# Output product of the feed-forward part as split one-pass products with stationary weights, its tail in the next group, and loads two groups ahead

## The reference, cut to what matters

```python
x = _layernorm(x + mixer(x))          # inner width 256, 4 heads of 64
x = _layernorm(x + ffn(x))
# ffn, on tokens xf (8192 x 128), 16 experts of hidden width 64, one shared of width 128:
g = sigmoid(xf @ gate_w.T)
topv, topi = top_k(g, 4)
combine = zeros_like(g).at[rows, topi].add(topv / sum(topv))
hin = einsum('td,edh->eth', xf, e_win)
vin = einsum('td,edh->eth', xf, e_vin)
h = silu(hin) * vin * combine.T[:, :, None]
routed = einsum('eth,ehd->td', h, e_wout)
shared = silu(xf @ ws_in) * (xf @ vs_in) @ ws_out
ffn = shared + routed
```

## Time and profile before

| what | us |
|---|---|
| median of 3 runs (912.12 to 923.52) | 912.57 |
| profiled execution, its own time | 916.93 |
| its span, first to last instruction | 915.2 |
| TensorE busy | 823.2 |
| VectorE busy | 669.4 |
| GpSimd busy | 372.1 |
| ScalarE busy | 363.3 |
| mean granted TensorE clock, as a share of 2.4 GHz | 0.966 |

### The profile page before, as it was taken

The page is one execution under the profiler, slowest core; times in us unless marked ns, Lnnn a source line. Parts: engine busy times, 40 slices in busy tenths (PEclk is TensorE's granted clock), DMA queues, the critical chain, the costliest instruction groups (busy, mean ns, idle before and its releaser), DMA issues.

```text
span 915.2 us, 17726 instructions
## 1 busy us (share of the span) xinstructions
PE 823.2 (90%) x5783; PEld 643.9 (70%) x5783; DVE 669.4 (73%) x1759; ACT 363.3 (40%) x621; POOL 372.1 (41%) x372
## 2 busy tenths in 40 slices
PE   6879866799999999899989999999999999999966
PEld 5646655677777777777777777777777777777754
DVE  5899944577777777777786878777867777878654
ACT  4767742224343434333333443333434343433131
POOL 5040037253536262626262626353726353534200
PEclk8999977699999999999999999999999999999979
DMA  4877734300403040404030403040304040400000
GB/s 114 258 242 271 272 116 119 115 25 24 126 23 126 24 126 23 126 23 126 23 126 23 126 23 126 23 126 23 126 23 126 23 126 23 126 23 24 1 11 12
DMA packets 53104, 81.01 MB, mean 89 GB/s; under 512 B 10176, under 2 KB 36952, under 8 KB 49112
## 3 DMA queue, kind: packets, MB, share of 16 engines
q1 hardware_dynamic: 53080, 80.68, 28.2%
HBM read 55.24 MB, written 25.43 MB: 88 GB/s over the span
## 4 chain that ended last, share of the span: by engine, by line
PE 49%; DVE 17%; issue 14%; DMA 10%; POOL 5%; SPq 3%; ACT 2%; POOLq 1%; DVEq 0%; ACTq 0%
PE bank L1402 12%; DMA max_b<-max_scratch 7%; PE bank L1372 5%; PE bank L1376 5%; PE bank L1373 5%; PE bank L1392 4%; PE bank L1345 3%; DVE st L991 3%; PE bank L1321 3%; DVE acc L839 2%; PE bank L1319 2%; DVE Y L1003 2%; PE bank L1326 2%; DMA x_in<-in_L_attn_x_dram 2%; DVE out_sb L1003 2%
## 5 line engine op out<-in xcount | busy, mean ns | idle before, releaser
L755 ACT ACTIVATE s_in<-bank 128x512 f32<-128x512 f32 x144 | 85.9, 597 | 195.9 <-PE bank L1376 195.0
L1402 PE MATMUL bank<-ewout,h 128*128 128x128 f32 x1024 | 146.5, 286 | 0.0
L1402 PEld LDWEIGHTS bank<-ewout,h 128*128 128x128 f32 x1024 | 123.9, 191 | 25.4 <-issue 25.4
L554 POOL TENSOR_TENSOR rs<-ve,half 128x4 f32<-128x4 f32 x32 | 32.6, 1019 | 267.5 <-DVE ve L999 267.5
L1103 DVE TENSOR_TENSOR h<-s_in,bank 128x512 f32<-128x512 f32 x144 | 98.1, 681 | 58.5 <-PE bank L1376 50.3
L1372 PE MATMUL bank<-yT_hi,in_hi 128*128 128x512 f32 x288 | 128.2, 445 | 6.8 <-DVE h L1103 6.8
L1376 PE MATMUL bank<-yT_lo,in_hi 128*128 128x512 f32 x288 | 115.3, 400 | 0.0
L1373 PE MATMUL bank<-yT_hi,in_lo 128*128 128x512 f32 x288 | 114.6, 398 | 0.0
L540 POOL TENSOR_TENSOR D<-a_tok,max_b 128x512 f32<-128x512 f32 x64 | 65.4, 1043 | 118.5 <-DVE max_b L911 67.9
L1107 DVE TENSOR_TENSOR h<-h,bank 128x512 f32<-128x512 f32 x128 | 87.3, 682 | 19.8 <-PE bank L1392 19.8
L952 DVE TENSOR_TENSOR state<-kept,bank 64x130 f32<-64x130 f32 x128 | 36.6, 286 | 64.8 <-POOL kept L569 34.7
(11 more groups left out here) (197 smaller groups left out, 1634.2 us busy)
## 6 DMA issues: line engine op xcount, KB each, us to landing
xact_scratch<-xact SPq DMA_DIRECT2D x16, 1024.0 KB, 4.9
max_b<-max_scratch SPq DMA_DIRECT2D x15, 1024.0 KB, 7.7
xa<-xact_scratch SPq DMA_DIRECT2D x16, 512.0 KB, 6.4
silu_z<-xact_scratch SPq DMA_DIRECT2D x16, 512.0 KB, 3.8
inter_w<-inter_scratch SPq DMA_DIRECT2D x30, 256.0 KB, 7.0
x_in<-in_L_attn_x_dram SPq DMA_DIRECT2D x16, 256.0 KB, 4.9
xt_scratch<-x_t SPq DMA_DIRECT2D x16, 256.0 KB, 4.8
xT<-xt_scratch SPq DMA_DIRECT2D x16, 256.0 KB, 8.0
```

The costliest lines, as they stand in the source:

```text
L755: act.activation(s_in[:, j % 2], bank[4][:], ACT.Silu).then_inc(silu_done, 1)
L1402: i = pe.matmul(bank[7][:, k * P:(k + 1) * P], h2[:, j % 2, k * P:(k + 1) * P], w, start=(j == k == 0), stop=(j == NJ), skip_group_check=True)
```

## The change

- The output product has the weights as the stationary operand and h as the moving one: out^T = w^T h, in three one-pass products of 128x512 (`ffn_out_high`: out_hi x h_hi, out_lo x h_hi; `ffn_out_low`: out_hi x h_lo, a slot later), summed in bank 7. GpSimd splits the output weights in phase 1.
- h2 gets a ring of RB = 4 buffers. ScalarE makes its rounded part h_hi (`hidden_high`), GpSimd the rest h_lo (`hidden_low`), nine times a group each.
- The output is now transposed: ScalarE copies bank 7 to oT (`out_copy`), TensorE transposes it back (`out_tokens`), into bank 6. This tail, the sum with Y (kept by ScalarE in y_res), its statistics and its normalisation are done in the next call of `mix`: `ffn_sum` in slot 1, `ffn_statistics` in slot 2, `ffn_norm` in slot 6, ahead of the mixer step of that slot. So each group's result is stored one group later.
- The head's transposes use bank 5 instead of bank 7.
- The combine weights are split in two f32r parts instead of three bf16 ones (routing has eleven operations), with 128 rows in the combine product. `combine_rows(j - 1)` stands between the two halves of `ffn_in(j)` from slot 3.
- VectorE's slot order is h2(j - 1) first, then h1(j), but for slot 2.
- The skip products go from GpSimd to ScalarE. GpSimd's order is written out by hand anew, with the differences and masks of the two halves apart.
- `max_b` is loaded two groups ahead; the loop runs over groups 2 to 13, with 1 and 14 written out.

```diff
             def mix(g, f):        # SyncE
-                sp.wait_ge(arg_sub, nth(g, 4, 3))
-                if not (isinstance(g, int) and g == NG - 1):
-                    load_max(g + 1)
+                if not is_last(g):
                     sp.wait_ge(val_mm[1], g + 1)
...
+                if f is not None and before(f) is not None:
+                    store(before(f))
+                if not is_last(g, 2):
+                    sp.wait_ge(arg_sub, nth(g + 1, 4, 3))
+                    load_max(g + 2)
...
+                keep_state(0)
+                keep_state(1)
+                hidden_low(f, 0)
+                if more:
+                    arg_differences(g + 1, 0, 0)
+                    arg_differences(g + 1, 0, 1)
+                keep_state(2)
+                hidden_low(f, 1)
+                if more:
+                    arg_mask(g + 1, 0, 0)
+                    arg_mask(g + 1, 0, 1)
+                keep_state(3)
+                hidden_low(f, 2)
+                normalised(0)
+                hidden_low(f, 3)
+                normalised(1)
+                if f is not None and before(f) is not None:
+                    norm_power(before(f))
+                hidden_low(f, 4)
+                if more:
+                    arg_differences(g + 1, 1, 0)
+                    arg_differences(g + 1, 1, 1)
+                hidden_low(f, 5)
+                if more:
+                    arg_mask(g + 1, 1, 0)
+                    arg_mask(g + 1, 1, 1)
+                for j in range(6, NJ + 1):
+                    hidden_low(f, j)
                 pool.wait_ge(ve1_done, g + 1)
                 power(rs1[:], ve1[:], rs1_done)
-                if f is not None:
-                    ffn(f)
-                if not (isinstance(g, int) and g == NG - 1):
+                if more:
                     weigh_queries(g + 1)
...
             def ffn_slot(f, j):        # ScalarE
                 if j == 2:
                     act.wait_ge(combT_mm, f + 1)
-                    copy(combT[:], bank[6][0:3 * NX, 0:G // 2].bitcast(BF16)).then_inc(combT_out, 1)
+                    prev(act, bc_mm, f, NJ)
+                    copy(combT[0:2 * NX], bank[6][0:2 * NX, :]).then_inc(combT_out, 1)
+                if j:
+                    hidden_high(f, j - 1) if j != 2 else None
                 act.wait_ge(hin_mm, nth(f, NJ + 1, j))
                 if j >= 2:
                     act.wait_ge(h1_done, nth(f, NJ + 1, j - 2))
                 act.activation(s_in[:, j % 2], bank[4][:], ACT.Silu).then_inc(silu_done, 1)
+                if j == 2:
+                    hidden_high(f, 1)
...
+            def hidden_high(f, j):
+                if j:
+                    act.wait_ge(h2_done, nth(f, NJ, j - 1))
...
+                copy(h_hi[:, j % RB], h2[:, j % RB]).then_inc(h_hi_done, 1)
...
                 for j in range(NJ + 2):        # VectorE
                     if f is not None:
                         ffn_slot(f, j)
+                    if f is not None and before(f) is not None:
+                        if j == 1:
+                            ffn_sum(before(f))
+                        elif j == 2:
+                            ffn_statistics(before(f))
+                        elif j == 6:
+                            ffn_norm(before(f))
                     for what, arg in DVE_SLOT.get(j, ()):
...
             def ffn_slot(f, j):
+                if j == 2:
+                    hidden(f, j)
                 if j >= 2:
+                    weigh_hidden(f, j - 1)
+                if j <= NJ and j != 2:
+                    hidden(f, j)
...
                 for m, (done, free) in enumerate(((hin_mm, silu_done), (vin_mm, h1_done))):
+                    if m and j >= 3:
+                        combine_rows(f, j - 1)
...
+            def ffn_out_high(f, j):
+                pe.wait_ge(h_hi_done, nth(f, NJ + 1, j))
+                if j == 0:
+                    prev(pe, oT_done, f)
+                pe.matmul(bank[7][:], out_hi[:, j], h_hi[:, j % RB], start=(j == 0), stop=False)
+                pe.matmul(bank[7][:], out_lo[:, j], h_hi[:, j % RB], start=False, stop=False).then_inc(out_hi_mm, 1)
+
+            def ffn_out_low(f, j):
+                pe.wait_ge(h_lo_done, nth(f, NJ + 1, j))
+                pe.matmul(bank[7][:], out_hi[:, j], h_lo[:, j % RB], start=False, stop=(j == NJ)).then_inc(out_lo_mm, 1)
...
-                if 2 <= j <= NJ + 1:
+                if j == 2 or j == NJ + 1:
                     combine_rows(f, j - 1)
-                if j >= 2:
-                    ffn_out(f, j - 2)
+                if 2 <= j <= NJ + 2:
+                    ffn_out_high(f, j - 2)
+                if 3 <= j <= NJ + 2:
+                    ffn_out_low(f, j - 3)
```

More of the change, by code:

```diff
@@ L323, in groups, with before, is_last @@
             mix(0, None)
-            with eng.Fori(1, NG - 1) as g:
+            mix(1, 0)
+            with eng.Fori(2, NG - 2) as g:
                 mix(g, g - 1)
+            mix(NG - 2, NG - 3)
             mix(NG - 1, NG - 2)
             ffn(NG - 1)
+        def before(f):
+            return None if isinstance(f, int) and f == 0 else f - 1
+        def is_last(g, n=1):
+            return isinstance(g, int) and g >= NG - n
         def prev(eng, s, g, per=1):
@@ L514, in _ @@
             i.then_inc(blocks_made, 1)
-            halves = pair_rows[:].rearrange("r j (t m) -> r j t m", t=P // HX)
-            for part in range(3):
+            halves = pair_f[:].rearrange("r j (t m) -> r j t m", t=P // HX)
+            for part in range(2):
                 pool.affine_select(out=halves, in_=halves, compare_op=ALU.not_equal, fill=1.0, base=-NX * part,
@@ L563, in mix, with keep_state @@
                 dec = decay[:].rearrange("p s (g k) -> p g k s", k=NC)[:, bass.ds(g, 1)].rearrange("p g k s -> p (g k) s")
-                for k in range(NC):
+                more = not (isinstance(g, int) and g == NG - 1)
+                def keep_state(k):
                     if k:
@@ L702, in mix_front, with decays @@
                      bank[3][:].rearrange("p (q d) -> p q d", d=DH)).then_inc(val_out[0], 1)
-            def decays(g):
-                for q in range(4):
+            def decays(g, first=0, last=4):
+                for q in range(first, last):
                     act.wait_ge(arg_masked, nth(g, 4, q))
@@ L716, in mix @@
                         ffn_slot(f, j)
+                    if j == 1:
+                        act.wait_ge(xa_in, 16 * (g + 1))
+                        prev(act, down_mm, g)
+                        for p in range(NP):
+                            act.activation(mixed[:, p], xa[:, p], ACT.Copy, scale=vecs[:, p, VS:VS + 1]
+                                           ).then_inc(skip_done, 1)
+                    if j == 5 and f is not None:
+                        keep_y(f)
                     if j in U_SLOT:
@@ L734, in mix @@
                 if not last:
-                    decays(g + 1)
+                    decays(g + 1, 0, 2)
+                if f is not None:
+                    hidden_high(f, NJ)
+                if not last:
+                    decays(g + 1, 2, 4)
                 if not last:
@@ L740, in ffn_head @@
                 act.wait_ge(yT_mm, f + 1)
-                prev2(act, z2_done, f)
-                copy(yT[:], bank[7][:]).then_inc(yT_out, 1)
-                copy(yT_hi[:], bank[7][:]).then_inc(yT_hi_done, 1)
+                copy(yT[:], bank[5][:]).then_inc(yT_out, 1)
+                copy(yT_hi[:], bank[5][:]).then_inc(yT_hi_done, 1)
+                if before(f) is not None:
+                    out_copy(before(f))
                 act.wait_ge(logit_mm, f + 1)
@@ L1035, in mix @@
                 mixer_out(g)
-                if f is not None:
-                    ffn_sum(f)
                 mixer_norm(g)
@@ L1425, in mix @@
                         ffn_slot(f, j)
+                    if j == 0 and f is not None and before(f) is not None:
+                        pe.wait_ge(ge_done, f + 1)
+                        out_tokens(before(f))
                     for what, arg in PE_SLOT.get(j, ()):
@@ L1428, in mix @@
                             if arg is not None else head_transposes(g)
-                if not (isinstance(g, int) and g == NG - 1):
-                    mix_front(g + 1)
+                last = isinstance(g, int) and g == NG - 1
+                if not last:
+                    mix_keys(g + 1)
+                if f is not None:
+                    ffn_out_low(f, NJ)
+                if not last:
+                    mix_values(g + 1)
             def ffn(f):
```

235 lines of the change are left out of this document (145 added, 90 removed).

## The result

| what | before | after |
|---|---|---|
| median of 4 runs each, us | 918.01 (912.12 to 923.52) | 1063.07 (1057.91 to 1065.71) |
| profiled execution: span, us | 915.2 | 1056.2 |
| mean granted TensorE clock | 0.966 | 0.911 |
| mean of the 14 groups of the loop, head to head, us | 46.49 | 55.65 |

The change makes the kernel slower: ratio 1.1575, 95% interval 1.1465 to 1.1684. The forecast was 1003 with a range of 930 to 1035: right in its direction, too low in its size, and outside its range.

The account below looks back on a forecast made before the run. TensorE bounds the kernel before; after, a VectorE-ScalarE chain decides. Period 39.15 + 12.45 + 1.0 = 52.6 us, +6.2 on 46.43; in sum +91 on 916.9 = 1008, 4.4 lower for the median: 1003, range 930 to 1035.

Parts of the forecast that it names:

- The chain: Slot to slot: three products, combine, weigh, rounding, Silu take 2.99 us, against 2.30 of TensorE's own work.
- the signs named as right: Slots 3 to 8 at least 2.9 us, slot 7 stand 4 to 6, clock under 1.0, normalisations 0.7 or more, heads 51 to 54.
- Rival (a): TensorE stays the bound and VectorE's queue keeps up: 40.6 us a group, 838 to 850 in all; chance 0.11.
- Rival (b): Slower but mildly, nothing held by GpSimd and the clock stays: period 48.7, about 945; chance 0.18.
- what GpSimd holds: VectorE beside GpSimd's 1.04 us operations: four normalisations take 3.2 instead of 1.1, the second head scale is partly held.
- the clock: TensorE from slot 8, behind the stand: low clock costs 0 to 2.5 us a group, 1.0 taken.
- Rival (d): The low clock reaches through slots 8 to 10 and the front each time: period 55, about 1035; chance 0.04.
- the sum over the groups: Group 1 +1, groups 2 to 14 +81, group 15 +1.5, last feed-forward +5, group 0 -1, phase 1 +3.5: +91.
- max_b: Loads two groups ahead remove GpSimd's wait for that transfer, which lies behind work: no gain counted.

Follow-up runs that it names:

- Experiments 1: The kernel after, with ScalarE's rounding of slot j-1 behind the Silu of slot j in every slot: 993.54 us.
- 2: The kernel after, with the four moved normalisations, and the store behind them, at the end of mix behind yT_low: 1035.94 us.
- experiment 4: The kernel after, with hidden_low over 32 of the 512 tokens and the rest of h_lo zero: 995.35 us.
- experiment 6: The kernel before, with only the max_b load moved two groups ahead: 944.0 us against 916.35 beside it.
- Experiment 10: The kernel after, with the gate products of slot 7 made six times: 1047.26 us, ratio 1.1403 to the kernel before.
- 3: The kernel after, with GpSimd waiting for Y before it weighs the next queries: 1042.72 us.
- 5: The kernel after with three edits together (Silu ahead of rounding, normalisations at the group's end, next queries weighed behind Y): 897.75 us.
- 7: The kernel before, with the combine weights in two f32r parts and the combine product in f32r: 885.18 us in one execution.
- 11: The kernel before with two-part combine weights and an f32r combine product, in timed rounds: 887.22 us, ratio 0.9641.
- experiment 12: The kernel before with two-part f32r combine weights, and GpSimd's differences and masks placed where VectorE isn't in routing: 875.55 us, ratio 0.9528.

## Why the prediction was right in its direction and wrong in its size

**The chain was right.** In t from the head at 567.09, with the forecast behind: slot 4 at 21.64 (20.6), slot 5 at 24.76 (23.6), slot 6 at 29.72 (27.95), slot 7 at 32.94 (31.2), slot 8 at 41.09 (39.15). The stand is 5.58 (5.7), and 4.0 to 4.6 where slot 6 has the low clock. Of the signs named as right all came but the last: heads are 55.65 apart, not 51 to 54. Slot 3 starts at 15.67 (16.0), the cycle of a plain slot is 3.12 (2.99), gating takes 2.5 and the normalisations 3.36 (3.2). Experiments 1 and 2 show both halves of the reason: rounding ahead of Silu, and the moved normalisations. Rival (a), TensorE stays the bound, falls with the first timeline; only after three edits is TensorE near it. Rival (b) adds up to some 950, not 945 (912.6 + 30 + 7).

**First failed step: what GpSimd holds** ("partly held by GpSimd's hidden_low", and "1.04 each for the two-tensor ones"). The prediction counted the hold in full at one place, the four normalisations, and in part at the second head scale, and took `hidden_low` for the row of `hn`. It takes 1.28, and with the mask that it pushes back it holds the first operation of each head scale and the last of the statistics, 0.66 to 1.10 where 0.17 is bare. Slot 3 so takes 5.97 us where 4.6 was forecast. The starts are late by 1.04 at slot 4, 1.77 at slot 6 and 1.94 at slot 8. With a small `hidden_low` slot 8 starts at 37.4 (the prediction had 37.1 "without any blocking"): 3.7 us ahead of the kernel after, where the prediction had allowed 2.1 for the hold, so by this measure 1.6 of the 1.94 are this step. Over the whole group experiment 4 gives 4.4; it shortens GpSimd's own queue too, so that is hold and queue together. The Trainium skill (Advanced Engine Details and Errata, VectorE Performance Modes) says that VectorE's second SBUF port is shared with GpSimd, and that GpSimd instructions and VectorE's two-port instructions block each other. The runs show holds beside GpSimd (3.36 for 1.11, 1.00 for 0.58; in experiment 6 in every group); which of VectorE's instructions used two ports no run shows.

**Second: the clock** ("I take 1.0, since waits take part of it"). Experiment 10 measures 1.9, or 1.6 between its own groups. The tail, from slot 8 to the next head, was 14.31 us against 12.45 + 1.0; without the 1.9 it is 12.4, so its other terms came out right in sum. With the 1.94 ahead of slot 8 and the clock's 0.9, the period is 52.6 + 2.8 = 55.4, which is the group shown. Rival (d) had that period, 55, but for another reason: it laid the whole difference on the clock, which carries 0.9 of it. It got 4% of the chances.

**Third: the sum over the groups** ("Group 1 has no tail of an earlier group in it: +1", "Group 15 ... +1.5", "The last feed-forward alone ... +5"). Group 1 took 54.70, 5.9 more than before: without a tail it still has the chain, the hold and the low clock. Group 15 gave +3.5, the last part +7.6 (its slots are 3.2 us apart, each waiting 0.58 for a Silu). Together that is 4.9 + 2.0 + 2.6 = 9.5 us, and 13 groups at about 3.2 more are 41. The rest, +1.8 for start and phase 1, was taken as +2.5. The sum comes to the 50 by which 141 exceeds 91. The other 10 of the 60 between 1003 and 1063.07 lie in the executions: the forecast took off 4.4 us for the profiled one before, and the median after lies 5.2 above its own.

**Fourth: max_b** ("take away the wait for that transfer, behind work in my count"). The prediction priced it at nothing, and read the wait of 1.73 in one of the four groups in which the differences came early. Experiment 6 shows that the wait for the transfer did useful work, 1.6 us a group on the kernel before. In the kernel after it is hardly seen, since the wait on routing is 0.39 there; what it costs in that order wasn't tried.

**The range** took its upper end from (d). In hindsight it should have joined the ends of the unknown terms, all of which point the same way: slots later by 2 us for further holds, and a full clock loss of 2.5 for 1.0, give 52.6 + 2 + 1.5 = 56 a group.

**What stays open.** Why three edits give 10.7 where they sum to 7.4 is only argued: slot 8 keeps the low clock in 1, 2 and 3 and has the full clock in 5, and experiment 10 prices that at 1.6 to 1.9 us a group, but the share of the clock in the difference wasn't measured apart. Experiments 1 to 7 rest on one execution each (7 was repeated as 11). Nor was it tried how experiment 12 would do with the new output product.

## What to carry to other kernels

Before work is moved to an idle engine, go through each in-order queue for what the new instruction stands in front of: here one copy ahead of a Silu and four normalisations ahead of the operation that frees a bank turned a busy TensorE into a waiting one. Price GpSimd's operations by what VectorE does beside them, and put them where VectorE isn't in a chain of short operations that another engine waits for, such as routing; a load brought forward can lose that protection. When single edits disappoint, try them together: the waits replace each other.

## What the hardware showed that was not expected

Added TensorE work made the kernel faster: 15 products more a group, 15.8 us less in all. Waits of one length were followed by either clock: the 2.2 to 2.4 us ahead of slot 6 by the low clock in ten groups of the kernel after and by the full clock in four, and the 2.50 us of experiment 6 by the low clock in four groups and by the full clock in most. The low clock in slot 6 was mostly free, since it shortened a stand; the one in slot 8 cost 1.6 to 1.9 us. A VectorE operation on 8 elements a partition took 1.10 us beside GpSimd's `hidden_low`, 0.17 without. And of GpSimd's two differences of 128x512 the one written as f32r (`hidden_low`) took 1.28 us, the one written as f32 (D) 1.03.
